# Sixty-four and seventy semaphore increments ahead of VectorE's two attention loops

## The reference

```python
h = (x @ W).reshape(n, heads, ch)
e = alpha_src[src] + alpha_dst[dst]
e = jnp.where(e > 0, e, NEG_SLOPE * e)
alpha = _segment_softmax(e, dst, n)
msg = h[src] * alpha[:, :, None]
out = jax.ops.segment_sum(msg, dst, num_segments=n)
```

## Time and profile before

| What | Value |
|---|---|
| median of 3 runs | 8885.42 us (8884.1 to 8887.7) |
| profiled execution | 8883.06 us, span 8881.5 us |
| busy, share of the span | TensorE 71%, VectorE 69%, GpSimd 70%, ScalarE 55% |
| granted TensorE clock, mean | 0.776 |
| loop of attention layer 1 on VectorE | 4112.3 to 6445.4 us, ends of the first and the last turn |
| loop of attention layer 2 on VectorE | 6657.4 to 8810.9 us, ends of the first and the last turn |

### The profile page before, as it was taken

One profiled execution on the slowest core, in us unless ns is written; L12 is line 12 of the kernel. 1 busy time (PEld: TensorE's weight loads), 2 busy tenths in 40 slices (PEclk: granted clock), 3 DMA queues, 4 the chain that ended last, 5 costly groups with the idle time before them and its releaser, 6 DMA issues.

```text
span 8881.5 us, 230954 instructions
## 1 busy us (share of the span) xinstructions
PE 6275.0 (71%) x50513; PEld 5141.0 (58%) x50514; DVE 6144.7 (69%) x25661; ACT 4847.3 (55%) x11867; POOL 6174.0 (70%) x7562
## 2 busy tenths in 40 slices
PE   2466666666599999986666666666667777777775
PEld 2365655566588888874444444444455556555655
DVE  7799833333267777768888888888866666666665
ACT  4133333333245555546666666666657777777775
POOL 0377777777777777737777777777747777777775
PEclk9988888888899999988888888888855555555555
DMA  4232232222233333312222222222332212112114
GB/s 141 52 63 62 62 64 62 63 62 62 61 90 85 86 85 86 85 54 55 53 53 53 53 54 53 53 53 53 52 31 29 29 29 29 29 29 29 29 29 29
DMA packets 991593, 495.78 MB, mean 56 GB/s; under 512 B 831203, under 2 KB 842005, under 8 KB 990677
## 3 DMA queue, kind: packets, MB, share of 16 engines
q0 software_dynamic: 168832, 302.29, 15.6%
q1 hardware_dynamic: 702292, 169.41, 10.0%
q10 hardware_dynamic: 119840, 18.68, 1.3%
HBM read 356.46 MB, written 151.48 MB: 57 GB/s over the span
## 4 chain that ended last, share of the span: by engine, by line
issue 29%; PE 19%; DVE 18%; POOL 17%; ACT 7%; DMA 5%; DVEq 4%; ACTq 1%; POOLq 0%; SPq 0%
POOL z_s L649 13%; PE ps_all L987 5%; PE ps_all L997 5%; POOL arena L699 4%; DMA arena<-table,arena 4%; PE ps_all L1010 3%; ACT arena L851 3%; DVE arena L1552 3%; PE ps_all L1007 2%; DVEq L387 1%; DMA z_s<-arena 1%; ACT arena L883 1%; PE ps_all L1019 1%; PE ps_all L1095 1%; DVE arena L1638 1%
## 5 line engine op out<-in xcount | busy, mean ns | idle before, releaser
L699 POOL DMA_INDIRECT arena<-table,arena x3616 | 3509.7, 971 | 1438.8 <-issue 929.8
L649 POOL DMA_INDIRECT z_s<-arena x1660 | 1592.4, 959 | 850.6 <-issue 483.5
L1119 PE MATMUL ps_all<-arena 128*128 128x132 f32 (+1 forms) x7232 | 1548.6, 382 | 1.8 <-DVE acc L1655 1.8
L1119 PEld LDWEIGHTS ps_all<-arena 128*128 128x128 f32 x7232 | 1375.1, 282 | 2.6 <-issue 2.6
L851 ACT ACTIVATE arena<-lanes_b,arena 128x128 bf16<-128x128 bf16 x3616 | 1147.1, 387 | 415.9 <-DVE arena L1525 405.3
L1552 DVE TENSOR_REDUCE arena<-ps_all 128x2 f32<-128x1024 f32 x904 | 1100.6, 1218 | 14.1 <-PE ps_all L1136 14.1
L1136 PE MATMUL ps_all<-arena,pick 128*128 128x512 bf16 x2260 | 934.3, 500 | 134.2 <-DVE arena L1552 133.6
L1107 PE MATMUL ps_all<-arena 128*128 128x8 bf16 (+1 forms) x10848 | 434.2, 168 | 761.4 <-DVE arena L1629 737.0
L1095 PE MATMUL ps_all<-ident_b,arena 128*128 128x128 bf16 x3616 | 457.9, 267 | 691.5 <-DMA arena<-table,arena 486.7
L754 ACT ACTIVATE arena<-ps_all 18x512 f32<-18x512 f32 x415 | 243.6, 587 | 1215.3 <-PE ps_all L974 1194.1
L1107 PEld LDWEIGHTS ps_all<-arena 128*128 128x128 bf16 x10848 | 399.7, 104 | 854.9 <-DVE arena L1629 762.5
(11 more groups left out here) (268 smaller groups left out, 15227.4 us busy)
## 6 DMA issues: line engine op xcount, KB each, us to landing
arena<-z_s SPq DMA_DIRECT2D x452, 264.0 KB, 2.6
arena<-table,arena POOLq DMA_INDIRECT x3616
arena<-rec_d SPq DMA_DIRECT2D x1660, 10.0 KB
z_s<-arena POOLq DMA_INDIRECT x1660
rec_d<-in_rec ACTq DMA_DIRECT2D x1, 16160.0 KB, 59.6
arena<-ids_d SPq DMA_DIRECT2D x904, 4.0 KB
arena<-pos_d SPq DMA_DIRECT2D x830, 0.5 KB
arena<-pos_d ACTq DMA_DIRECT2D x830, 0.5 KB
```

The lines of the kernel that those rows point to most:

```text
L649: pool.indirect_dma_start(z_s, bass.IndirectOffsetOnAxis(ap=slot[:, g.slot(SLOTS), u:u + 1], axis=0), z_out[:, g.slot(SLOTS), u, :], None) ...
L699: pool.indirect_dma_start(g_rows[:, r, u * step + CODE_WORDS:(u + 1) * step], None, tables[n], bass.IndirectOffsetOnAxis(ap=ids[:, r, 0, u ...
L1119: mm = pe.matmul(ps[6][:, 0:out_w], a_hot_f[:, g.slot(4), u, :], g_msg[:, g.slot(4), u * out_w:(u + 1) * out_w], start=(u == 0), stop=(u = ...
```

## The change

In layer 1 64 and in layer 2 70 semaphore increments stand on VectorE ahead of the written-out first groups. The semaphore that they add to, `go`, is waited for by nobody. To have a semaphore free for it, `turned_clear` is given up: TensorE doesn't wait for it any more, and the memset at L1430 goes through `link`, so that VectorE waits for it ahead of its next step.

```diff
+LOOP_AT = (64, 70)
...
                 pe.wait_ge(S("sums_started"), before + len(BATCHES))
-                pe.wait_ge(S("turned_clear"), 1)
                 pe.wait_ge(S("codes_in"), 1)
...
-            dve.memset(turned[:, :, 1, :], 0.0).then_inc(S("turned_clear"), 1)
+            link(dve.memset(turned[:, :, 1, :], 0.0))
...
                 dve.wait_ge(S("sums_started"), before + len(BATCHES))
+                for _ in range(LOOP_AT[n]):
+                    dve.sem_inc(S("go"), 1)
```

## The result

| | before | after |
|---|---|---|
| median | 8886.05 us (9 runs) | 8912.64 us (9 runs) |
| lowest to highest | 8883.29 to 8888.75 | 8907.52 to 8915.62 |
| ratio | | 1.003, 95% interval 1.0021 to 1.004 |
| profiled execution | 8883.06 us, span 8881.5 | 8914.76 us, span 8913.2 |

The change makes the kernel slower by 0.3%, with 0.21% as the low end of the interval. The time lies in the forecast range, 8878 to 8925 us, but above its likeliest part, which ended at 8901 and had a chance of 0.62: it lies where the milder form of the second rival was put. The likeliest figure, 8896 us, had the right mechanism with about half of its size.

What follows compares the result with a forecast made beforehand. The prediction took VectorE to bound loop 1 and GpSimd loop 2. Loop 1's crossings added 12.7 us and the other terms 0 to the profiled 8883.06 us, giving 8896 us, range 8878 to 8925.

Steps and rivals of the forecast that it cites:

- likeliest part: Whole kernel: 8880 to 8901 us, within 0.2% of before, chance 0.62.
- second rival: Loop 1: L1524 waits 2.9 us each turn, 9037 us, chance 0.05; milder, 0.34 to 1.39 us, 0.19 above 8901.
- VectorE sets loop 1, GpSimd loop 2: Attention loops: VectorE sets loop 1's 44.0 us a turn, GpSimd loop 2's 40.6 us.
- Stretches of 128 from 64 above a multiple of 128: VectorE's program: fetched in stretches of 128 instructions starting there; both loops touch four, fitting five packets a turn.
- The rule weighed: Instruction fetch: the skill's blocks of 256 with two held, against the trace's 128 with four; same forecast sum either way.
- The changed loops still lie in four: Both attention loops: still touch four stretches after the change, so the 2.9 us a turn stay.
- Term 1: Loop 1: stretch crossings move to places 12, 140 and 268, costing +0.24 us a turn, +12.7 us.
- Term 2: Loop 2: moved crossings change a few tenths a turn, hidden behind GpSimd; 0.
- Term 3: Ahead of both loops: increments of 0.075 us each, 4.8 and 5.2 us, covered; 0, at most 20 us.
- Term 4: Memset at L1430: VectorE's next step waits for it, TensorE loses a wait long over; 0.
- The sign of the second rival: Loop 1: the wait at L1524 passing 0.5 us decides for the milder form.
- The first rival: Both loops lie in three stretches, queue 14 falls silent, loop 1's turn falls to 41.1 us: 8727 us, chance 0.14.

Runs made afterwards that it cites:

- places 44 and 45: Loop 1 moved by (120, 77), then (121, 77) increments instead of the change's (64, 70); ratio 0.9957 on the 11903.41 us chip, then 8926.78 us.
- places 20: Both loops moved to the 20th place of a stretch by (96, 72) increments instead of the change's (64, 70); 8724.39 us, ratio 0.9825.
- same-places run: (128, 129) increments instead of the change's (64, 70), so both loops keep the places in a stretch they had before the change; 8881.02 us.

## Why the prediction was right, and where it fell short

- **VectorE sets loop 1, GpSimd loop 2**: right. Taking away loop 2's stall alone moves nothing (8876.98 us), loop 1's alone moves nearly everything (8726.12 us).
- **Stretches of 128 from 64 above a multiple of 128**: right, shown by places 44 and 45 with 69 and 600 packets. That three stretches stay for a loop is shown by them too. That four are held and one of them is fetched ahead is the reading that fits 5 packets a turn; no run tests it by itself.
- **The rule weighed**, by the two edges that were found later: blocks of 256 don't fit with either parity. With starts at 2112 and 2368, loop 1 would lie in two blocks at 2156 and at 2157 alike, and only the first is free of the stall; with starts at 1984 and 2240, the kernel before (2036 to 2375) would be free of it, and isn't.
- **The changed loops still lie in four**: right, 252 and 249 packets and the 3.9 us ahead of L1580.
- **Term 1, loop 1's crossings, +0.24 us a turn**: the mechanism was right and the size half. At place 12 I had 0.45 us, measured 0.51, a mean of turns with the plain 0.37 and turns in which the packet comes later. At 140 I had 0.1, measured 0.03. At 268 I had 0.1, measured 0.34: L1585 shows only 1.8 us in 9 waits, the rest is L1652 starting late behind it. What was removed I took from the waits as 0.41; it was 0.33 + 0.27 = 0.60 less 0.10 that VectorE gave back in another wait. Head of turn to head of turn it comes to 44.34 against 43.95, +0.39 us, 20.2 us over the 52 such distances.
- **The rest of loop 1 was not in the sum at all**: in the last turn the stall and the crossing last far longer. From its jump's first instruction to its branch that turn took 51.0 us, before 44.6, so 6.4 us once. That the total still fell into the range is thus partly luck: its upper end allowed for a larger wait in each turn, not for one long turn. The timeline of VectorE after shows it, with the same place before (second fence):

```profile
6421.82 0.16 DVE L1580 TENSOR_SCALAR arena<-dst_parts 128x12 bf16 x1 [6.69 <-issue]
...
6429.71 0.17 DVE L1524 TENSOR_TENSOR arena<-arena,first_node 128x8 int32<-128x8 int32 x1 [7.51 <-issue]
```

```profile
6402.40 0.16 DVE L1578 TENSOR_SCALAR arena<-dst_parts 128x12 bf16 x1 [6.58 <-issue]
...
6402.92 0.17 DVE L1522 TENSOR_TENSOR arena<-arena,first_node 128x8 int32<-128x8 int32 x1
```

  The stall is 6.69 us, before 6.58; but L1524 then waits 7.51 us, since in the last turn the second stretch comes late too: its packet on queue 14 starts 9.3 us after the first's, where in a middle turn it was 2.5 us. In the kernel before the second packet is late in that turn too, by 7.4 us instead of 2.5, but is not needed until place 76. Why packets are late in that turn was not tried. A long last turn isn't the refetch's doing by itself: with both loops in places 20 it takes 51.9 us against 40.6 for the others, without a packet in it, and VectorE waits for TensorE instead.
- **Term 2**: loop 2 grew by 2.9 us in all, put at 0. The ways from loop 1 to loop 2 and from loop 2 to the end grew by 1.5 us each, which no term had; neither was followed.
- **Term 3, the increments**: right that they cost nothing on the path (8881.02 with 257 of them). Each took 0.09 us where I had 0.075:

```profile
L1506 DVEq EVENT_SEMAPHORE  x64: 21/21/50, 3985.1 to 3990.9; - x64
...
L1506 DVEq EVENT_SEMAPHORE  x70: 21/21/49, 6568.3 to 6574.7; - x70
```

- **Term 4**: 0, as far as the same-places run and the one without increments tell.
- **The sign of the second rival** was a wait of over 0.5 us at L1524; it is 0.63, of which 0.14 was there before.
- **The first rival**, put at 8727 us, had the right price for the wrong place: 8724.39 us when the loops do fit. **The second** is where the result lies, in its milder form, from 8901 to 8957 us, to which I had given 0.19. Its full form, 2.9 us at L1524, is out, since the second stretch is usable some 2.55 us after the jump's first instruction, 0.5 us after the turn asks for it. But its mechanism holds in part: the second packet does start only after the jump's first instruction.

## What to carry to other kernels

Before padding a loop to a boundary, find the boundary in the trace: the pauses that no semaphore explains, each set against the number of the instruction behind it, counted in the built program with everything that the engine executes and without labels. A loop is worth moving when it lies in one stretch more than can be held and its engine sets the pace; a move that leaves it in as many stretches can lose, as here, where (76, 72) or (96, 72) increments gain 1.5 and 1.8% and (64, 70) lose 0.3%. When pricing such a move, price all crossings, by what stands behind each, and not only the first.

## What the runs showed of the hardware

- VectorE's program comes in stretches of 128 instructions (8.2 KB a packet). A loop within three stretches jumps back in 0.23 us (0.20 on the chip with 11903.41 us), one that touches a fourth, if only with its branch, in 2.8 to 3.8 us in the mean.
- The stretch behind the target of such a jump is usable 2.55 us after the jump's first instruction in the mean, 2.34 to 3.03 in single turns, and only after 7.9 and 9.4 us in the last turn of two kernels; 1.1 to 1.5 us lie between its packet's end and the instruction that waits.
- Beside that, entering a stretch costs 0.3 to 0.4 us among short instructions, on every pass of a loop of four stretches. The Trainium skill, "Runtime: NRT & Kernel Launch", section "Instruction fetch mechanics", calls the cost of crossing a block mostly hidden. Here it is hidden only behind a long instruction.
- On one chip the kernel before took 11903.41 us instead of some 8880, with a mean granted TensorE clock of 0.70 instead of 0.78. The four changed kernels profiled there are busy 6098 to 6114 us on VectorE and 6132 to 6151 on GpSimd, against 6145 and 6174 in the kernel before on the other chip, so the time went into waiting; why was not looked into.
